# Conditional projection and quantised FFN on one core: the order of the steps laid out anew on all five queues

## The reference

```python
w = weight[ids]                                   # (8, 1024, 1024)
y = jnp.einsum('bij,bkj->bik', x, w)              # x: (8, 256, 1024)
h = layernorm(y) * gamma + beta
h = fq(h) @ fq(w1).T + b1                         # fq: s = max|row|/127, round(row/s) * s
h = gelu(h)
h = fq(h) @ fq(w3).T + b3
return x + h
```

## Time and profile before

| | |
|---|---|
| Median of 3 runs | 369.0 us |
| All runs | 373.23, 369.0, 368.7 us |
| Span of the profiled execution | 372.5 us |
| TensorE busy | 341.4 us (92%) |
| VectorE busy | 285.5 us (77%) |
| POOL busy | 263.4 us (71%) |
| ScalarE busy | 227.1 us (61%) |
| Moved by DMA | 67.35 MB, 181 GB/s over the span |

### The profile page before, as it was taken

The page is one execution under the profiler, slowest core; times in us unless marked ns, Lnnn a source line. Parts: engine busy times, 40 slices in busy tenths (PEclk is TensorE's granted clock), DMA queues, the critical chain, the costliest instruction groups (busy, mean ns, idle before and its releaser), DMA issues.

```text
span 372.5 us, 5769 instructions
## 1 busy us (share of the span) xinstructions
PE 341.4 (92%) x1854; PEld 235.9 (63%) x1880; DVE 285.5 (77%) x344; ACT 227.1 (61%) x232; POOL 263.4 (71%) x164
## 2 busy tenths in 40 slices
PE   6898899996976999999999999999899989999885
PEld 6787788754763666666665666566566666674442
DVE  1459698886946777798778886888779687999866
ACT  2433476854888647773777658755777477625651
POOL 1402259841998579995999599968997699946831
PEclk9999999999899999999999999999999999999989
DMA  6999998695950899539971999099925990150014
GB/s 186 352 347 352 410 280 164 147 246 117 241 99 0 199 276 218 100 119 294 221 154 63 299 223 203 0 268 244 220 56 158 288 229 0 58 171 1 0 55 172
DMA packets 46203, 67.35 MB, mean 181 GB/s; under 512 B 2918, under 2 KB 37734, under 8 KB 46186
## 3 DMA queue, kind: packets, MB, share of 16 engines
q1 hardware_dynamic: 46186, 67.14, 68.8%
HBM read 58.74 MB, written 8.39 MB: 180 GB/s over the span
## 4 chain that ended last, share of the span: by engine, by line
POOL 41%; issue 22%; DMA 13%; DVE 11%; PE 7%; SPq 3%; ACT 2%; POOLq 0%; DVEq 0%
POOL y L458 8%; POOL x_res L474 7%; POOL o L466 6%; POOL y L460 5%; DMA x_res<-in_L_ffn_w 5%; POOL a L478 4%; POOL x_lo L483 4%; POOL o L469 3%; DMA w_scale_row<-in_L_ffn_w 3%; PE t_ps L1134 2%; DMA h_r<-in_L_cond_weight 2%; DVE x_nat L917 2%; DMA x_t<-in_L_ffn_b 2%; DVE wq_max L861 2%; DMA w_nat<-in_L_cond_weight 2%
## 5 line engine op out<-in xcount | busy, mean ns | idle before, releaser
L1080 PE MATMUL a_ps<-w_hi,x_hi 128*128 128x512 f32 x256 | 107.5, 420 | 2.4 <-DVE w_lo L794 1.2
L1082 PE MATMUL a_ps<-w_hi,x_lo 128*128 128x512 f32 x256 | 100.8, 394 | 0.0
L1081 PE MATMUL a_ps<-w_lo,x_hi 128*128 128x512 f32 x256 | 100.7, 393 | 0.0
L1134 PE MATMUL f_ps<-w_q,q_t 128*128 128x512 bf16 x377 | 88.1, 379 | 9.7 <-ACT q_t L627 8.2
L1134 PEld LDWEIGHTS f_ps<-w_q,q_t 128*128 128x128 bf16 x400 | 37.1, 98 | 57.5 <-ACT q_t L627 12.5
L803 DVE STREAM_TRANSPOSE t_ps<-w_nat 128x1024 f32<-128x1024 f32 x48 | 57.5, 1238 | 11.7 <-DMA w_nat<-in_L_cond_weight 11.5
L809 DVE TENSOR_TENSOR w_lo<-t_ps,w_hi 128x1024 fp32r<-128x1024 f32 x48 | 57.2, 1219 | 8.9 <-ACT w_hi L574 8.7
L574 ACT ACTIVATE w_hi<-t_ps 128x1024 fp32r<-128x1024 f32 x48 | 49.0, 1023 | 21.9 <-DVE t_ps L803 21.1
L1080 PEld LDWEIGHTS a_ps<-w_hi,x_hi 128*128 128x128 f32 x256 | 48.5, 189 | 15.7 <-ACT y L589 3.2
L1082 PEld LDWEIGHTS a_ps<-w_hi,x_lo 128*128 128x128 f32 x256 | 48.5, 189 | 10.7
L1081 PEld LDWEIGHTS a_ps<-w_lo,x_hi 128*128 128x128 f32 x256 | 48.6, 190 | 9.0
(11 more groups left out here) (151 smaller groups left out, 503.1 us busy)
## 6 DMA issues: line engine op xcount, KB each, us to landing
w_nat<-in_L_cond_weight SPq DMA_DIRECT2D x96, 256.0 KB, 6.5
x_res<-in_x SPq DMA_DIRECT2D x7, 1024.0 KB, 6.3
out<-o SPq DMA_DIRECT2D x14, 512.0 KB, 3.1
x_nat<-in_x SPq DMA_DIRECT2D x24, 256.0 KB, 9.9
w_nat<-in_L_cond_weight SPq DMA_DIRECT2D x10, 512.0 KB, 8.9
w_q<-in_L_ffn_w SPq DMA_DIRECT2D x4, 512.0 KB, 7.9
h_r<-in_L_cond_weight SPq DMA_DIRECT2D x4, 512.0 KB, 6.7
w_scale_row<-in_L_ffn_w SPq DMA_DIRECT2D x3, 512.0 KB, 10.3
```

What stands on the lines that cost most here:

```text
L1080: pe.matmul(ps, hi, w_hi[:, u, c], start=begin, stop=False)
L1081: pe.matmul(ps, hi, w_lo[:, u, c], start=False, stop=False)
L1082: last = pe.matmul(ps, lo, w_hi[:, u, c], start=False, stop=end)
L1134: last = pe.matmul(ps[:, half, :], q[:, c, :], w[:, c, half_of(half)], start=c == 0, stop=c == CB - 1)
```

## The change

Only the lists are changed. On each queue the same steps stand in another order, no step is added or taken out, and no function of a step is changed. In the loop, SyncE's and TensorE's lists stay as they are; ScalarE's, VectorE's and POOL's are new. In the stretch for the first three sequences all five lists are new. The diff for the loop, and the head and two other places of the first stretch:

```diff
 # POOL, period(p)
                 residual(p - 1)
+                low_x(p + 1, 1)
                 normalisers_of(p)
-                low_x(p + 1, 1)
                 add_b1(p - 1, 1)
 # ScalarE, period(p)
-                both(p + 1, 0)
+                split_w(p + 1, 0, 0)
                 take_h(p - 1)
+                split_w(p + 1, 0, 1)
                 split_x(p + 1, 0)
-                both(p + 1, 1)
+                split_w(p + 1, 1, 0)
                 gelu(p - 1, 0)
                 copy_y(p, 1)
+                split_x(p + 1, 1)
+                split_w(p + 1, 1, 1)
                 round_g(p - 1, 0)
-                split_x(p + 1, 1)
+                split_w(p + 1, 2, 0)
                 normalise(p, 0)
-                normalise(p, 1)
-                split_w(p + 1, 2, 0)
                 take_g(p - 1, 0)
                 gelu(p - 1, 1)
                 split_w(p + 1, 2, 1)
+                normalise(p, 1)
+                scale_ffn2(p - 1, 0)
                 round_g(p - 1, 1)
-                scale_ffn2(p - 1, 0)
+                split_w(p + 1, 3, 0)
+                split_w(p + 1, 3, 1)
+                take_g(p - 1, 1)
                 round_h(p, 0)
-                split_w(p + 1, 3, 0)
-                take_g(p - 1, 1)
-                split_w(p + 1, 3, 1)
                 round_h(p, 1)
 # VectorE, period(p)
-                both(transpose_w, p + 1, 0)
-                both(low_w, p + 1, 0)
+                transpose_w(p + 1, 0, 0)
+                transpose_w(p + 1, 0, 1)
                 transpose_x(p + 1)
-                both(transpose_w, p + 1, 1)
+                low_w(p + 1, 0, 0)
+                low_w(p + 1, 0, 1)
                 rescale1(p - 1, 0)
-                both(low_w, p + 1, 1)
+                transpose_w(p + 1, 1, 0)
+                transpose_w(p + 1, 1, 1)
+                low_w(p + 1, 1, 0)
                 scales_g(p - 1, 0, a[:, 0, :], 0)
                 statistics(p, 1)
                 mean_and_variance(p)
+                transpose_w(p + 1, 2, 0)
                 rescale1(p - 1, 1)
-                both(transpose_w, p + 1, 2)
+                low_w(p + 1, 1, 1)
                 low_w(p + 1, 2, 0)
+                transpose_w(p + 1, 2, 1)
                 scales_g(p - 1, 1, a[:, 1, :], 1)
                 low_w(p + 1, 2, 1)
+                transpose_w(p + 1, 3, 0)
+                transpose_w(p + 1, 3, 1)
                 scales_h(p, 0, 0)
-                both(transpose_w, p + 1, 3)
                 scales_h(p, 1, 1)
-                both(low_w, p + 1, 3)
+                low_w(p + 1, 3, 0)
+                low_w(p + 1, 3, 1)
 # SyncE, first stretch
             sp.wait_ge(ids_loaded, 16)
+            load_prep((2,))
             load_first_unit(0)
...
 # TensorE, first stretch, around the transposes of w3's first tiles
-            piece(1, 2, 1)
+            piece(1, 3, 0)
             ffn1(0, 0)
-            piece(1, 3, 0)
+            piece(1, 3, 1)
             ffn1(0, 1)
-            piece(1, 3, 1)
-            prepare((9, 10))
+            prepare((9,))
+            prepare((10,))
             piece(2, 0, 0)
             prepare((11,))
+            prepare((12,))
+            prepare((13,))
             piece(2, 0, 1)
-            prepare((12, 13))
+            prepare((14,))
+            prepare((15,))
             piece(2, 1, 0)
-            prepare((14, 15))
+            scale_row(1)
             piece(2, 1, 1)
-            scale_row(1)
```

More of the change, by code:

```diff
@@ L495, in period @@
                 residual(p - 1)
+                low_x(p + 1, 1)
                 normalisers_of(p)
-                low_x(p + 1, 1)
                 add_b1(p - 1, 1)
-                for t in range(TT):
-                    scale_and_shift(p, t)
-                for t in range(TT):
-                    finish(p - 1, t)
+                scale_and_shift(p, 0)
+                scale_and_shift(p, 1)
+                finish(p - 1, 0)
+                finish(p - 1, 1)
             pool.memset(ident[:], 0.0).then_inc(consts_zeroed, 1)
@@ L518, in _ @@
                 pool.partition_broadcast(rows[:, k], rows_1[k]).then_inc(rows_ready, 1)
-            round_prep((0, 1, 2, 3, 4, 5, 6))
+            round_prep((0,))
+            round_prep((1,))
+            round_prep((2,))
+            round_prep((3,))
+            round_prep((4,))
+            round_prep((5,))
+            round_prep((6,))
+            round_prep((7,))
+            round_prep((8,))
             normalisers_of(0)
-            round_prep((7,))
             scale_and_shift(0, 0)
-            round_prep((8,))
             scale_and_shift(0, 1)
-            round_prep((9, 10, 11, 12))
+            round_prep((9,))
+            round_prep((10,))
+            round_prep((11,))
+            round_prep((12,))
             low_x(2, 0)
@@ L529, in _ @@
             round_prep((13,))
+            round_prep((14,))
+            round_prep((15,))
+            normalisers_of(1)
             low_x(2, 1)
-            round_prep((14, 15))
-            normalisers_of(1)
             residual(0)
@@ L1009, in _ @@
             low_first(6)
+            low_first(7)
+            low_first(8)
             max_prep((0, 1))
-            low_first(7)
             max_prep((2, 3))
-            low_first(8)
             low_first(9)
             scales_prep(0)
+            low_first(10)
+            statistics(0, 0)
             max_prep((4,))
-            low_first(10)
             max_prep((5, 6))
@@ L1021, in _ @@
             max_prep((7, 8))
+            scales_prep(1)
             low_first(13)
             low_first(14)
-            scales_prep(1)
-            statistics(0, 0)
             statistics(0, 1)
@@ L1028, in _ @@
             mean_and_variance(0)
+            max_prep((9, 10, 11, 12))
             low_first(16)
-            max_prep((9, 10, 11, 12))
-            scales_prep(2)
             low_first(17)
             scales_h(0, 0, 0)
+            transpose_x(2)
             low_first(18)
-            transpose_x(2)
             low_first(19)
+            scales_prep(2)
             scales_h(0, 1, 1)
-            both(transpose_w, 2, 0)
+            transpose_w(2, 0, 0)
+            transpose_w(2, 0, 1)
+            statistics(1, 0)
             low_w(2, 0, 0)
+            low_w(2, 0, 1)
             transpose_w(2, 1, 0)
-            statistics(1, 0)
-            low_w(2, 0, 1)
+            transpose_w(2, 1, 1)
             low_w(2, 1, 0)
             rescale1(0, 0)
-            transpose_w(2, 1, 1)
             transpose_w(2, 2, 0)
@@ L1050, in _ @@
             scales_prep(3)
+            statistics(1, 1)
+            scales_g(0, 0, a[:, 0, :], 0)
+            mean_and_variance(1)
             low_w(2, 1, 1)
-            scales_g(0, 0, a[:, 0, :], 0)
-            statistics(1, 1)
-            mean_and_variance(1)
+            low_w(2, 2, 0)
             transpose_w(2, 2, 1)
-            low_w(2, 2, 0)
-            scales_g(0, 1, a[:, 1, :], 1)
             transpose_w(2, 3, 0)
@@ L1060, in _ @@
             transpose_w(2, 3, 1)
+            scales_g(0, 1, a[:, 1, :], 1)
+            low_w(2, 3, 0)
+            low_w(2, 3, 1)
             scales_h(1, 0, 0)
-            both(low_w, 2, 3)
             scales_h(1, 1, 1)
```

106 lines of the change are left out of this document (61 added, 45 removed).

## The result

The changed kernel takes 361.33 us, the median of four runs (360.34 to 362.2); the kernel before took 371.12 us in the same job (four runs, 368.7 to 472.58, the last far outside). The ratio is 0.9757, 95% interval 0.9717 to 0.9797: faster by 2.4%. The forecast was 361.0, in a range of 357.0 to 367.5. The profiled execution took 362.2 us with a span of 360.4, 12.1 less than the span shown before.

What follows compares the result with a forecast made beforehand. TensorE, busy 92% of 372.5 us, was taken as the bound. Gains of 6.2 (loop), 0.7 and 1.3 (first sequences) and 0.4 (tail) sum to 8.6, taken as 8.0 off the 369.0 median: 361.0 us, range 357.0 to 367.5.

Steps and rivals of the forecast that it cites:

- The order inside a round: Loop: steps of VectorE, ScalarE and POOL laid out by durations, removing TensorE's q_t and y waits; loop gains 6.2 us.
- The floor of a round is its 39.56 us less gaps of 1.14, 38.4: Loop: TensorE's order untouched, so removing its recorded gaps shortens a round to 38.4 us at best.
- Landed at about +18.1: Loop: unit 2 of the next weights lands about +18.1 us into the round; VectorE wants it at +17.4.
- That delays rescale1 of tile 1 to +20.9 and costs nothing: Loop: unit 2's landing delays rescale1 to +20.9, free because POOL takes its add_b1 at +21.8.
- rival 2: Loop: unit 2 lands later than +19.2, POOL slips, loop gains 2 to 4 us; time 364.2, chance 0.13.
- ScalarE runs take_g only at 186.26, since both normalises and a split stand before it: Loop, kernel before: ScalarE's order makes take_g late, with a 0.45 us gap before ffn2 of the first tile.
- First product at about 15.9: First stretch: TensorE's first product starts at about 15.9 us, not 12.26, behind two more transposes and later-landing weights.
- rival 4: First stretch: one landing comes 3 us earlier and both gates with it; time 357, chance 0.08.
- Gain 0.7, bounds 0.3 loss and 2.0 gain: First stretch: gain of 0.7 us from the prep tile that landed at 57.29, landing bounded between 54 and 57.3.
- The loop starts 28.8 after rescale1: Before the loop, behind prep tile 13's gate: loop starts 28.8 us after rescale1, not 30.1; 1.3 us gained.
- Rival 3, the clock: Start of kernel: gaps between transposes lower the clock, up to 23 us more; 377.5 at 17 us lost, chance 0.05.
- The tail, 0.4: After the loop: VectorE enters 0.6 us earlier, starting with two additions of 6.74 us against POOL; gain 0.4 us.

Runs made afterwards that it cites:

- e7: Changed kernel with SyncE's load of unit 1 of sequence p + 2 issued ahead of the store of tile 0 in the loop: 358.58 us.
- e11: Kernel before with one loop edit, the load of unit 1 two sequences ahead issued ahead of the first store: 364.18 us, ratio 0.9827.
- e5: The kernel before, unchanged, run again for a second profile: 368.94 us, span 367.1 us.
- e2: Kernel before with the changed kernel's five lists of the first stretch, old loop lists: 365.4 us, ratio 0.9872.
- e6: Kernel before with the load of unit 1 of sequence 3 ahead of the first store, end of first stretch: 370.62 us, ratio 0.9989.
- e9: Changed kernel with ScalarE's old list in the loop: 375.34 us, ratio 1.013 to the kernel before.
- e10: Changed kernel with POOL's old list in the loop: 361.63 us, ratio 0.9775 to the kernel before.
- e1: Kernel before with the changed kernel's loop lists on VectorE, ScalarE and POOL: 366.83 us, ratio 0.9884.
- e4: Changed kernel with SyncE's old list of the first stretch: 371.67 us, ratio 1.004 to the kernel before.

## Why the prediction was right, and where not

**The order inside a round: right.** In the last round before the tail (start 271.59), where the transfers have caught up, the steps come where they were laid out: rescale1 ends at +11.0 (laid out +10.8), add_b1 starts at +11.1 (+11.0), shift is ready at +22.1 (+21.8), take_g ends at +24.3 (+24.0), round_g at +31.0 (+30.9), and take_g of tile 1 at +33.7 (+33.7). The thinnest slack held: transpose_g starts at +31.2 with no wait. The rows for three of these:

```profile
294.89 1.00 ACT L646 ACTIVATE q_t<-f_ps 128x1024 bf16<-128x1024 int16 x1
...
301.34 1.23 ACT L641 ACTIVATE a<-a,magic,g_inv 128x1024 f32<-128x1024 f32 x1
...
304.28 1.03 ACT L646 ACTIVATE q_t<-f_ps 128x1024 bf16<-128x1024 int16 x1
```

**"The floor of a round is its 39.56 us less gaps of 1.14, 38.4": wrong.** It is 37.8: four rounds of e7 take 37.82. The idle time that the trace records ahead of a matmul is less than what the wait costs, since the modelled end of the matmul before it reaches past the point where the next could start: in the rows below the last product ends at 226.36, and the next matmul starts at 226.20. Ahead of ffn2, from the start of the last product to that of the first ffn2 matmul, it is 0.23 us in e7, where nothing waits:

```profile
225.97 0.39 PE L1116 MATMUL a_ps<-w_hi,x_lo 128*128 128x512 f32 x1
226.20 3.63 PE L1168 MATMUL f_ps<-w_q,q_t 128*128 128x512 bf16 x15
229.49 0.57 PE L1114 MATMUL a_ps<-w_hi,x_hi 128*128 128x512 f32 x1
```

The last product of the kernel before ahead of ffn2 of tile 0:

```profile
186.48 0.39 PE L1082 MATMUL a_ps<-w_hi,x_lo 128*128 128x512 f32 x1
```

ffn2 starts at 187.31, 0.83 us later: the wait cost 0.60 and is recorded as 0.45. From ffn2 to the next unit 2 it is 3.29 us in e7 and was 3.93: 0.64 against a recorded 0.30. With 0.54 for 0.39 at the third place, the round's waits cost 1.78, not 1.14. The stake in the loop was 198.83 - 5 x 37.82 = 9.7 us, not 6.7.

**"Landed at about +18.1": wrong by up to 2.2 us.** Unit 2 was there at +19.3, +20.3 (174.14), +19.7, +18.9 and +18.6 in the five rounds. I read its landing off the rates of the trace before, where the megabyte of unit 1 and the residual came ahead of it, and they still do. The reading was off as well: the slices near 400 GB/s end at 173.5 and not at 175, so the same sum should have given +16.6, still further from what came. "That delays rescale1 of tile 1 to +20.9 and costs nothing" failed with it: in the long round rescale1 of tile 1 ends at +22.9 and not at +20.9, and transpose_g, which no step of mine let wait for it, loses 0.98 us. All this is rival 2, whose mark was +19.2; the landing was past it in the first three rounds of five, though the first lost nothing by it, and the residual, which no step of mine priced, cost POOL up to 2.04 us beside it. What I took for the price (a loop that gains 2 to 4 us instead of 6.2, so 2.2 to 4.2 lost) is near what it took: 2.1 and 1.5 us in the second and third round and 0.8 in the fourth, by the rounds' lengths over 37.8, 4.4 in all. Stake and loss were both too small, and the loop's gain came to 5.4 where I had 6.2: that is near by luck. Two of my own signs of being wrong came true, rounds above 39.2 (39.9 and 39.3) and a wait for weights behind +19.2.

**"ScalarE runs take_g only at 186.26, since both normalises and a split stand before it": true of the row, wrong as a cause.** In e11 they stand there still, and the wait is gone. I had both links of the chain on paper, VectorE's 1.07 us for weights and POOL's 1.18 us behind it, and priced the reordering that steps around them. I did not ask who held the transfer: an issue behind a store that waits for the end of the round's chain on POOL.

**The first stretch.** "First product at about 15.9": it started at 14.14. The prep tile ahead of the first weights did not delay them by 1.5 us: their transposes start at 8.96, against 8.79 in the earlier trace rows. The start of the program, TensorE, after:

```profile
6.30 1.09 PE L1220 MATMUL t_ps<-ident,o 128*128 128x128 f32 x8 [0.98 <-DMA o<-in_x]
...
8.96 1.09 PE L1220 MATMUL t_ps<-ident,w_nat 128*128 128x128 f32 x8 [0.89 <-DMA w_nat<-in_L_cond_weight]
10.44 1.09 PE L1220 MATMUL f_ps<-ident,w_nat 128*128 128x128 f32 x8 [0.39 <-DMA w_nat<-in_L_cond_weight]
11.83 1.09 PE L1220 MATMUL t_ps<-ident,o 128*128 128x128 f32 x8 [0.29 <-DMA o<-in_x]
13.30 1.09 PE L1220 MATMUL t_ps<-ident,w_nat 128*128 128x128 f32 x8 [0.37 <-DMA w_nat<-in_L_cond_weight]
14.14 0.48 PE L1114 MATMUL a_ps<-w_hi,x_hi 128*128 128x512 f32 x1
```

From there to 63.4 TensorE is busy 49.09 of 49.20 us. Both gates at 57.29 and 88.08 are gone as gates, and TensorE reaches the transposes of prep tile 9 at 86.10 after a wait of 1.25 us, not 3. That both gates go together is what rival 4 said, to which I had given 0.08. What is left of the wait has another cause: VectorE waits 1.74 us for weights, until 81.17, ahead of rescale1 of tile 1. "Gain 0.7, bounds 0.3 loss and 2.0 gain" measured 5.8 between the two traces (91.89 to 86.10), outside the bounds; but most of that is the wait of 3.13 us and what followed it, which three of five traces of the old lists don't have. "The loop starts 28.8 after rescale1" measured 29.8 against 30.1: of the gain of 1.3 there came 0.3. The loop was entered at 115.9, not at 119.5 to 121. Of the four waits that e5 has between 104 and 114 (1.16, 1.62, 1.57, 1.12) three are left, and one for the copy of a prep tile is new. TensorE between 86 and 116, after:

```profile
86.10 1.05 PE L1145 MATMUL f_ps<-ident,x_res 128*128 128x128 bf16 x16 [1.25 <-DVE a L901]
91.63 0.61 PE L1145 MATMUL f_ps<-ident,w_scale_row 128*128 128x128 bf16 x8 [0.76 <-ACT w_q L658]
...
104.51 3.40 PE L1168 MATMUL f_ps<-w_q,q_t 128*128 128x512 bf16 x15 [1.34 <-ACT q_t L646]
109.21 0.61 PE L1145 MATMUL f_ps<-ident,a 128*128 128x128 bf16 x8 [1.30 <-ACT o L651]
110.93 5.31 PE L1168 MATMUL f_ps<-w_q,q_t 128*128 128x512 bf16 x16 [1.12 <-ACT q_t L646]
```

**Rival 3, the clock.** The granted clock was 1.00 up to 14.2 and from there to 63.4. Four gaps of 0.3 to 0.9 us between transposes did nothing to it.

**The tail, 0.4:** 0.6 between the two traces, 1.0 the other way against e5. The clock makes this difference: the granted clock falls to 0.50 for some 3 us in the last round of the changed kernel (343.5 to 346.5) and of the kernel before (356 to 359), and in e5's it stays at 1.00. Where it stays at 1.00, the last round takes 50.0 us with the old lists of the loop (e2, e5, e6) and 49.4 in e9 and e10, which have VectorE's new one. So the size was about right. The reason was not: VectorE starts its two additions at +1.4 of that round, where it had +1.5, and not 0.6 earlier. What changed is the price of the additions (below): e1 and e4 have the new lists of the loop and the old price, and their last rounds take 51.5 and 51.7 us, as the kernel before.

**The sum** of 8.0 in the median came to 8.5 to 9.8 by the jobs' own medians of before (369.9 to 371.1): the total was right, the loop's term nearly, the first stretch's by no working of mine. By the medians the loop's lists gave 3.1 to 4.1 of it and the first stretch 4.5 to 5.5, where I had some 6 and 2. That the sum came out is in good part luck.

## What to carry to other kernels

When a fixed list of steps has a wait in its middle, look first at the queue that issues the transfers, and at what stands ahead of the late one: here one load behind one blocked store cost 3 to 6 us, in the kernel before as in the changed one, and moving it gave as much as the new order of three engines. A stake in an engine's gaps is measured from start to start against an undisturbed round, not by adding recorded idle times. And two lists written for each other can't be tested one at a time: a half of the loop's change cost up to 5%.
